# A four-layer graph network on one core: TensorE's order in layers 1 and 2, one row's copies ahead of its neighbour's high part, one load two steps sooner

## The reference

```
layer 0: e = h @ h.T (h = x @ edge_w), where adj > 0; softmax over each row,
         times softmax(x @ node_w) over the nodes; (adj * att) @ (x @ weight) + bias
layer 1: e = exp(-leaky_relu(s_left[:, None] + s_right[None, :])) where adj; attn = e / sum(e)
         x_a = attn @ h; x_b = adj @ (x @ W_gcnb) + b; sigmoid(gate_a * x_a + gate_b * x_b)
layer 2: relu(norm(adj + I) @ (x @ weight))
layer 3: adj @ (relu(adj @ (relu(adj @ (x @ W1) + b1) @ W2) + b2) @ W3) + b3
after each layer:  x = layernorm(x + layer(x))
```

## Time and profile before

| | |
|---|---|
| runs | 761.91 us median of 3 (761.52 to 769.05) |
| the profiled execution | 762.32 us, of which the span of the core is 760.5 us |
| busy of TensorE, DVE, ACT, POOL | 733.7, 430.3, 345.2, 126.3 us |
| granted TensorE clock | 1.00 of full speed in all stretches after the start |

### The profile page before, as it was taken

One profiled execution on the slowest core, in us unless ns is written; L12 is line 12 of the kernel. 1 busy time (PEld: TensorE's weight loads), 2 busy tenths in 40 slices (PEclk: granted clock), 3 DMA queues, 4 the chain that ended last, 5 costly groups with the idle time before them and its releaser, 6 DMA issues.

```text
span 760.5 us, 12140 instructions
## 1 busy us (share of the span) xinstructions
PE 733.7 (96%) x4663; PEld 536.7 (71%) x4707; DVE 430.3 (57%) x893; ACT 345.2 (45%) x529; POOL 126.3 (17%) x253
## 2 busy tenths in 40 slices
PE   6999899998999999999999999999999999999997
PEld 5878788897779686877755556575664646467886
DVE  3586888797597897978954484033180311214533
ACT  4688977794574555547521153142260412224000
POOL 2111422112400011202123320000001000000443
PEclk9999999999999999999999999999999999999999
DMA  6997799988469139000030000000000000000011
GB/s 186 202 149 162 167 184 161 169 146 160 89 105 177 26 73 151 14 1 1 1 92 0 1 1 1 0 1 0 1 3 27 0 1 0 0 0 1 29 43 42
DMA packets 112916, 48.82 MB, mean 64 GB/s; under 512 B 102561, under 2 KB 108321, under 8 KB 112865
## 3 DMA queue, kind: packets, MB, share of 16 engines
q1 hardware_dynamic: 108464, 32.65, 21.4%
q0 software_dynamic: 4400, 15.47, 11.8%
HBM read 35.53 MB, written 2.10 MB: 49 GB/s over the span
## 4 chain that ended last, share of the span: by engine, by line
PE 48%; DVE 5%; issue 2%; ACT 1%; POOL 0%; POOLq 0%; DVEq 0%; ACTq 0%
PE ps L830 13%; PE ps L984 11%; PE ps L959 8%; PE ps L1030 6%; PE ps L993 3%; PE ps L942 3%; PE ps L1019 2%; PE ps L669 1%; DVE es_lo L1358 1%; DVE x L1662 1%; DVE tm L1582 1%; PE ps L1009 1%; DVE stats L1370 1%; DVE y L1624 0%; DVE nb L1579 0%
## 5 line engine op out<-in xcount | busy, mean ns | idle before, releaser
L830 PE MATMUL ps<-adjT,x 128*128 128x512 bf16 x736 | 167.8, 379 | 3.3 <-DVE x L1662 1.4
L830 PEld LDWEIGHTS ps<-adjT,x 128*128 128x128 f16 x768 | 72.5, 98 | 85.6 <-issue 1.7
L1358 DVE TENSOR_TENSOR hh_lo<-hf,hh_hi 128x512 fp32r<-128x512 f32 x32 | 22.2, 692 | 134.0 <-ACT hf L1293 133.0
L749 PE MATMUL ps<-sup,turned 128*128 128x256 f16 x768 | 86.6, 273 | 1.2 <-DMA turned<-pl 1.2
L984 PE MATMUL ps<-adjT,G 128*128 x375 | 82.6, 379 | 0.9 <-ACT hf L1293 0.4
L749 PEld LDWEIGHTS ps<-sup,turned 128*128 128x128 f16 x768 | 74.2, 98 | 12.4 <-issue 3.8
L874 PE MATMUL ps<-H_hi,es_hi 128*128 128x258 f32 x256 | 76.8, 300 | 2.2 <-DVE es_lo L1358 1.7
L874 PE MATMUL ps<-H_hi,es_lo 128*128 128x258 f32 x256 | 72.4, 283 | 0.0
L874 PE MATMUL ps<-H_lo,es_hi 128*128 128x258 f32 x256 | 72.4, 283 | 0.0
L984 PEld LDWEIGHTS ps<-adjT,G 128*128 128x128 f16 x384 | 37.3, 98 | 45.4 <-issue 0.9
L508 POOL TENSOR_TENSOR rstd<-mv,epsc 128x1 f32<-128x1 f32 x64 | 16.5, 258 | 275.0 <-DVE mv L1372 274.9
(11 more groups left out here) (233 smaller groups left out, 1422.9 us busy)
## 6 DMA issues: line engine op xcount, KB each, us to landing
adjb<-in_adj POOLq DMA_DIRECT2D x14, 512.0 KB, 7.1
adjf<-in_adj POOLq DMA_DIRECT2D x14, 512.0 KB, 7.0
out<-adjf SPq DMA_DIRECT2D x16, 128.0 KB, 1.7
x<-in_x SPq DMA_DIRECT2D x3, 512.0 KB, 7.1
adjf<-in_L_gnn_W SPq DMA_DIRECT2D x1, 1024.0 KB, 6.1
x<-in_x SPq DMA_DIRECT2D x2, 256.0 KB, 3.0
W1f<-in_L_gnn_W SPq DMA_DIRECT2D x1, 512.0 KB, 3.3
adjf<-in_L_gnn_W SPq DMA_DIRECT2D x1, 512.0 KB, 3.6
```

The costliest lines, as they stand in the source:

```text
L749: ins = mm(bank(6 + u, D), PT(part, t)[:, jt, :], sup[:, jt, c0:c0 + D], start=(jt == 0 and (part, c0) == (HI, 0)), stop=(jt == T - 1 and ...
L830: ins = mm(bank(agg_bank(layer, b, f)), x16[:, 1 - part, jt, f * P:(f + 1) * P], adj(b, jt), start=(jt == 0 and part == HI), stop=(jt == T ...
L1358: return tt(to, frm, high.bitcast(F32), ALU.subtract)
```

## The change

Three things change. (1) TensorE's order: at pair 0 of blocks 1 to 3 of layer 1 the products with `es_hi` stand first and wait for `ef_ready` alone, and those with `es_lo` follow; in layer 2's first block the low parts of the last four tiles stand one tile behind the high parts; the last `out2` goes by halves f. (2) ACT's `keep_row(4)` stands ahead of `p_high(3)`, and DVE's `maxima(4)` waits for row 2's `pl`. (3) Row 4's second load is issued at POOL's step 8, not 10.

```diff
-    LATER_LOADED = {10: 4}
+    LATER_LOADED = {8: 4}
...
+            def attend_first(b):
+
+                for low in (False, True):
+                    pe.wait_ge(es_lo if low else ef_ready, b * PAIRS + 1)
+                    for jt in (0, 1):
+                        for k in range(TB):
+                            if jt == 0 and not low:
+                                pe.wait_ge(z_ready, (b - 1) * TB + k + 1)
+                            for p, q in ((LO, HI),) if low else ((HI, HI), (HI, LO)):
+                                ins = mm(bank(k, D + 2), es[p][:, (b * T + jt) % RE, k * P:(k + 1) * P], H[q][:, jt, :],
+                                         start=(jt == 0 and (p, q) == (HI, HI)), stop=False)
+                ins.then_inc(e_used, 1)
...
-                    attend(b, pair)
+                    if b and pair == 0:
+                        attend_first(b)
+                    else:
+                        attend(b, pair)
...
+            def out2_last():
+
+                for f in range(KD):
+                    pe.wait_ge(agg_lo, (2 * B - 1) * KD + f + 1)
+                    for k in range(TB):
+                        if f == 0:
+                            pe.wait_ge(relu_ready, TB + (B - 2) * TB + k + 1)
+                        for p, q in ((HI, HI), (HI, LO), (LO, HI)):
+                            ins = mm(bank(k, D), agg[p][:, f, k * P:(k + 1) * P], wls[q][:, f, 0:D],
+                                     start=(f == 0 and (p, q) == (HI, HI)), stop=(f == KD - 1 and p == LO))
+                        if f == KD - 1:
+                            ins.then_inc(o2_mm, 1)
+
+            def last_tiles():
+
+                for jt in range(T - TB, T + 1):
+                    if jt < T:
+                        pe.wait_ge(conv_hi, T + jt + 1)
+                        for f in range(KD):
+                            mm(bank(agg_bank(1, 0, f)), x16[:, 1 - HI, jt, f * P:(f + 1) * P], adj(0, jt),
+                               start=False, stop=False)
+                    if jt > T - TB:
+                        pe.wait_ge(conv_lo, T + jt)
+                        for f in range(KD):
+                            ins = mm(bank(agg_bank(1, 0, f)), x16[:, 1 - LO, jt - 1, f * P:(f + 1) * P], adj(0, jt - 1),
+                                     start=False, stop=(jt == T))
+                            if jt == T:
+                                ins.then_inc(agg_mm, 1)
+
             pe.wait_ge(diag_added, TB)
-            for jt in range(T):
+            for jt in range(T - TB):
                 for f in range(KD):
                     aggregate_tiles(1, 0, f, (jt,))
+            last_tiles()
...
-            out2(B - 1)
+            out2_last()
...
             for t in range(2, T):
-                if t > TB - 1:
+                if t > TB:
                     keep_row(t)
...
                 exp_row(t)
+                if t + 1 == TB:
+                    keep_row(t + 1)
                 p_high(t)
...
                 dve.wait_ge(fill_ready, t + 1)
+                if t == TB:
+                    dve.wait_ge(p_lo, 2 * t - 2)
```

## The result

The change made the kernel slower: 769.67 us median of 18 runs (763.45 to 777.09) against 763.44 for before on the same chip (761.21 to 780.22). The ratio is 1.0092, 95% interval 1.0073 to 1.0111, so about 7 us more (5.6 to 8.5) where I had forecast 3.5 less. The profiled execution took 774.85 us with a span of 773.0, one of the longer ones; it shows the loss larger than the median has it.

A forecast was written before the change was run, and what follows sets the result against it. TensorE, busy 733.7 of 760.5 us, was taken to bound the kernel, so only idle time could be won. Layer 0's 2.4 + 0 + 0.69 + 0.4 = 3.5 us less gave 758.5 us, range 757.0 to 761.7.

The forecast's parts named there:

- Row 4's copies: Layer 0, row 5's scores: 1.9 us gained; price: p_high(3) and its transpose 1.45 us later, with 0.3 us to spare.
- What is late next?: Layer 0 after row 5: TensorE's lead of 1.9 us passes the following rounds; the tight place is round 13, slack 1.3 us.
- The third rival: Layer 0: row 3's high part slips through layer 1's weight loads, eating the 1.9 us; 760 to 761.2 us, chance 0.1.
- The place of the load: POOL's step 8: row 4's second load goes out at 146 to 147 us instead of 163.07.
- The landing of row 11's high part: Layer 0, ahead of p_high(12): beside the load it takes 7.1 us instead of 5.2, bounds 5.2 to 9.3.
- The estimate of 3.2 us for a load: Skill page's fit, 2.0 us plus bytes over 436 GB/s, for a 512 KB load; collision then 1.2 us or less.
- The other side, slower: SP's queue and DMA engines, 146 to 160 us: load served ahead of row 11's transpose; +1.5, 763.8 us profiled, chance 0.05.
- The low part of row 13: Layer 0, row 13's matmuls: without the load beside it, it lands 2.8 us sooner and TensorE's 1.23 us wait goes.
- Pair 0 in layer 1: Blocks 1 to 3: starting at ef_ready instead of es_lo is worth 0; bounds +0.1 to -0.3 us a block.
- Layer 2's tail: Layer 2's first block, last four tiles: the new order leaves no wait for tile 13's low part, gain 0.69 us.
- the last out2: Layer 2's end, out2 by halves: layer 3 starts 0.4 us sooner, not 1.4, as relu waits for three matmuls, not six.
- The rule that the prediction weighed: DMA engines take turns between queues with work, packet by packet, so a load beside a transpose stretches both.

The follow-up runs named there:

- the first kernel with the weights held: After, with POOL's loads of layer 1's weights held until the transpose of row 4's high part has landed: 770.82 us, ratio 1.0075 against before.

## Why the prediction was wrong

- **Row 4's copies: the gain and the price were right.** No wait at row 5's scores, `p_high(4)` at its old time, row 3's high part landed in 3.7 us.
- **"What is late next?" failed.** This is the step that failed first. I followed the lead through TensorE and the maxima and took every landing on the way, but for row 11's, as unchanged. What also moved was POOL: its steps hang on DVE's moments, and with them the weight loads. These are instructions that the change does not touch. The third rival named these loads, but for row 3's transpose, which had landed before them, and left out that the early copies move them; it was row 4's (9.3 us instead of 5.4). I gave that rival 760 to 761.2 us, 1 to 2 below before; the copies alone measured 2.1 us above before.
- **The place of the load was off.** I put it at 146 to 147 us; in the profile it went out at 154.85, since the chain was late by then. Alone it went out at 147.62 and cost 1.7 us.
- **The landing of row 11's high part was mis-sized.** This is the second step that failed, the term of 1.9 us (7.1 - 5.2) in the sum. I took 7.1 us, "since there the load followed the transpose by half a microsecond", with 9.3 as the end. It was 13.6 after and 8.9 with the load alone, 8.4 and 3.7 us above 5.2. The row at 9.3 was the nearer one: there load and transpose were 0.2 us apart, and the table puts the median within half a microsecond at 9.4. The estimate of 3.2 us for a load, which the sum did not use, also starts from too few bytes: `adj` is f32 in memory and the row is bf16 on the chip, so each load reads 1024 KB and writes the 512 KB of the earlier trace rows. The 58 adjacency loads of the traces with no other transfer beside them took 4.9 to 6.0 us, in the median 5.1.
- **The other side, slower, had the right place, and a price too small.** It decided from a landing of 10.7 us on and would have cost 1.5 us in all; it started from a chain that was on time. Here TensorE stood 7.40 us.
- **The low part of row 13** indeed stopped holding TensorE, as forecast; the 1.23 us are gone from the list. It didn't matter.
- **Pair 0 in layer 1: 0 was right.** With TensorE's order alone the wait for `es_lo` at pair 1 of block 3 fell from 0.75 us to 0.37, which I had not expected, but the pair itself took that much longer: from pair 0 to pair 1 it is 339.66 - 333.17 = 6.49 us, and 6.49 in before.
- **Layer 2's tail and the last out2 were right.** The 0.69 us of the earlier trace rows are gone. From the second half of the last out2 to layer 3 it is 453.38 - 450.49 = 2.89 us against 3.33 in the earlier trace rows: 0.4 us. Together with the tiles 1.1 us were forecast; the profiles show 1.1 to 1.2, and the time of TensorE's order alone fits it (0.5 to 4.3 us less).

Not settled: why six rounds of after run at 9.7 us each where before's take 8.6. The landings are the likely cause (rows 6 to 9 took 9.2, 8.2, 6.7 and 9.4 us; in before 7.1, 5.6, 8.1 and 9.3), and in each of these rounds a load lies within 2 us of the transpose. But before has such rounds too, no experiment moved these adjacency rows, and no run shows at which lateness the one rhythm turns into the other. Of after itself there is one profile, of a long run, so where a run near the median loses its time is open too. The spread of the runs (763 to 777 us) fits a collision that is met in some executions and missed in others: one experiment, whose order up to there is that of TensorE's order alone, had row 7's high part land in 10.7 us where that one had 6.2. Which runs hit and which miss was not profiled, and the profile of the copies with the load at step 8, with its 15.1 us at row 8, says that the place need not be row 11's.

## What to carry to other kernels

When a wait goes, list not only the chain that ran into it but everything that was timed by it: a queue that hangs on the same engine's later results, here POOL's by way of DVE's moments, moves as well, and its transfers meet others. Where the DMA engines are as busy as here (a share of 0.75 to 1.09 in the rounds from 97 to 150 us of before), the distance between two issues is part of the design; price a transfer moved to within half a microsecond of another by the worst row of the trace. A fix that shifts a burst of loads needs a free place to shift it to.

## What the hardware showed

Two things were new to me. First, some transfers that overlap don't only share the DMA engines: the engines are as busy and move less. Windows of before, of the first kernel with the weights held, and of the copies with the load at step 8; the last two columns are DMA share and GB/s:

```profile
100.00:120.00 20.00, 20.00 (x152) 17.33 (x151) 16.90 (x37) 15.38 (x19) 5.88 (x11) 1.00 1.00 186
```

```profile
100.00:120.00 20.00, 11.21 (x69) 9.44 (x69) 9.60 (x23) 6.84 (x8) 2.29 (x4) 0.83 1.22 107
```

```profile
120.00:140.00 20.00, 14.67 (x123) 12.55 (x123) 11.20 (x26) 8.70 (x13) 3.98 (x8) 0.96 1.23 103
```

A share of 1.00 moved 186 GB/s, one of 1.2 only 103 to 107. Not every overlap does this: before's window has row 6's transpose with a load issued 0.5 us behind it. In the last of them row 8's transpose and a load were issued 0.30 us apart and took 15.1 and 14.6 us. In after, row 11's two transposes and the load were all landed by 169.9, 15.4 us after the first was issued; alone they take some 3.7, 3.7 and 5.0 us, an estimate of 12.4 one behind the other.

The rule that the prediction weighed, from the Trainium skill ("DMA: Bandwidth & Descriptors", on queues, rings and completion order), that a DMA engine takes turns between queues, would have all of them land late together, as they did (167.98 to 169.92); it doesn't explain the 3 us more, nor the lower rate, and what does is open.

Second, the time that SP needs to issue a transpose is itself a sign of what is under way: 1.56 us for row 3's high part with nothing beside it, 3.87 beside the weight loads, 8.78 for row 11's low part behind two transfers under way. In none of the traces does SP issue anything else while it lasts. It doesn't tell what is to come: row 11's high part was issued in 1.56 us, and landed after 13.6.
